# Two pairs of PSUM banks that change places from image to image, and a GpSimd wait on VectorE, in a Winograd convolution block

## What is computed

```python
residual = x
out = conv3x3_decomposed(x, lsq_quantize(w1, alpha1))
out = jax.nn.relu(batchnorm(out, gamma1, beta1))
out = conv3x3_decomposed(out, lsq_quantize(w2, alpha2))
out = batchnorm(out, gamma2, beta2)
out = jax.nn.relu(out + residual)
```

## Time and profile before

| | |
|---|---|
| median of three runs | 1583.57 us (1582.01 to 1583.88) |
| the profiled execution | 1582.83 us, its span 1580.7 us |
| TensorE busy | 1112.5 us, 70% |
| VectorE busy | 1196.5 us, 76% |
| ScalarE busy | 842.3 us, 53% |
| GpSimd busy | 497.5 us, 31% |
| the steps | from 37.5 us to about 1265 us |
| the last stage | about 1265 us to the end |

### The profile page before, as it was taken

One profiled execution on the slowest core, in us unless ns is written; L12 is line 12 of the kernel. 1 busy time (PEld: TensorE's weight loads), 2 busy tenths in 40 slices (PEclk: granted clock), 3 DMA queues, 4 the chain that ended last, 5 costly groups with the idle time before them and its releaser, 6 DMA issues.

```text
span 1580.7 us, 22063 instructions
## 1 busy us (share of the span) xinstructions
PE 1112.5 (70%) x6954; PEld 1058.9 (67%) x6954; DVE 1196.5 (76%) x2074; ACT 842.3 (53%) x1135; POOL 497.5 (31%) x219
## 2 busy tenths in 40 slices
PE   5788998999999999579889999999989900000000
PEld 5787888888888888578888888888888900000000
DVE  7898998888888887688888888888888662323234
ACT  3454555555555555466766777776676552222224
POOL 2343334444433334133344444333344300000000
PEclk9998999999999999799999999999999955555555
DMA  4244444444442220001134444444222199999999
GB/s 191 84 164 161 164 163 163 163 163 180 181 182 107 81 81 1 1 41 82 81 122 163 163 183 180 177 184 189 103 81 81 51 419 430 429 430 430 430 430 407
DMA packets 28103, 296.89 MB, mean 188 GB/s; under 512 B 3888, under 2 KB 3888, under 8 KB 4784
## 3 DMA queue, kind: packets, MB, share of 16 engines
q1 hardware_dynamic: 22608, 245.25, 39.3%
q10 hardware_dynamic: 5472, 51.38, 7.6%
HBM read 174.59 MB, written 122.03 MB: 188 GB/s over the span
## 4 chain that ended last, share of the span: by engine, by line
DVE 42%; DMA 16%; PE 14%; issue 10%; DVEq 3%; ACT 2%; POOL 0%; POOLq 0%; ACTq 0%
PE conv_psum L942 13%; DMA slots<-conv_spill 10%; DVE slots L764 10%; DVE q_rows L696 8%; DVE v_rows L733 4%; DVE p_rows L721 4%; DVE d_lo L737 3%; DMA out<-slots 3%; DMA xbuf<-in_x 3%; DVE conv_psum L756 3%; DVE d L696 2%; DVE v_rows L696 2%; DVE slots L923 1%; DVE v_rows L717 1%; DVEq L764 1%
## 5 line engine op out<-in xcount | busy, mean ns | idle before, releaser
L454 POOL TENSOR_TENSOR v_lo<-v_rows,v_hi 128x1120 fp32r<-128x1120 f32 x192 | 494.9, 2592 | 751.8 <-ACT v_hi L513 751.8
L942 PE MATMUL conv_psum<-v_hi,w1T 128*128 128x284 f32 x1152 | 314.4, 301 | 69.2 <-DVE slots L764 62.5
L942 PE MATMUL conv_psum<-v_hi,w2T 128*128 128x284 f32 x1152 | 312.2, 299 | 66.5 <-DVE slots L764 58.9
L942 PE MATMUL conv_psum<-v_lo,w1T 128*128 128x284 f32 x1152 | 311.7, 299 | 0.0
L942 PE MATMUL conv_psum<-v_lo,w2T 128*128 128x284 f32 x1152 | 309.5, 297 | 0.0
L942 PEld LDWEIGHTS conv_psum<-v_hi,w1T 128*128 128x128 f32 x1152 | 222.0, 193 | 76.4 <-issue 70.5
L942 PEld LDWEIGHTS conv_psum<-v_hi,w2T 128*128 128x128 f32 x1152 | 220.7, 192 | 73.4 <-issue 63.2
L526 ACT COPY m<-conv_psum 128x568 f32<-128x568 f32 x128 | 81.3, 635 | 297.6 <-PE conv_psum L942 297.6
L556 ACT ACTIVATE squares<-slots,minus_shift 128x1120 bf16 (+3 forms) x192 | 223.5, 1164 | 28.8 <-DVE slots L764 15.1
L942 PEld LDWEIGHTS conv_psum<-v_lo,w1T 128*128 128x128 f32 x1152 | 222.6, 193 | 0.0
L942 PEld LDWEIGHTS conv_psum<-v_lo,w2T 128*128 128x128 f32 x1152 | 221.1, 192 | 0.0
(11 more groups left out here) (78 smaller groups left out, 1567.4 us busy)
## 6 DMA issues: line engine op xcount, KB each, us to landing
conv_spill<-slots SPq DMA_DIRECT2D x44, 1568.0 KB, 6.1
slots<-conv_spill SPq DMA_DIRECT2D x44, 1568.0 KB, 10.7
slots<-in_x SPq DMA_DIRECT2D x31, 1568.0 KB, 8.9
out<-slots ACTq DMA_DIRECT2D x30, 1568.0 KB, 11.6
xbuf<-in_x SPq DMA_DIRECT2D x28, 1568.0 KB, 52.8
xbuf_w<-in_x SPq DMA_DIRECT2D x4, 1568.0 KB, 51.9
out<-slots ACTq DMA_DIRECT2D x4, 784.0 KB, 10.3
slots<-in_L_conv_w SPq DMA_DIRECT2D x2, 576.0 KB, 9.7
```

The source lines that it names most:

```text
L454: nc.gpsimd.tensor_tensor(pair_window(1, k), pair_rows(k), pair_window(0, k).bitcast(F32), ALU.subtract).then_inc(lo_ready[k], 1)
L942: last = nc.tensor.matmul(bank_run(M_BANK[k] + grp, G_TILES), w[:, M_WEIGHT[k] + kw, :], run(v_plane[half][k // 2], r0, r0 + G_TILES, kw - 1),
```

## The change

`M_BANK` becomes a list for even images (b = 0) and one for odd ones (b = 1), and the chunks have no banks of their own list any more:

| banks (first of two) | k=0 | k=1 | k=2 | k=3 | k=4 | k=5 | chunks of the next image |
|---|---|---|---|---|---|---|---|
| before, every image | 2 | 4 | 6 | 0 | 4 | 6 | 2, 3 |
| after, even image | 2 | 4 | 0 | 6 | 4 | 2 | 2, 3 |
| after, odd image | 6 | 4 | 0 | 2 | 4 | 6 | 6, 7 |

So product 5 of image g and product 3 of image g + 1 now share banks, where product 5 shared them with product 2 before; and the chunks and product 5 of one step share banks. TensorE's waits follow: product 0 waits for the last sum of the image before, product 2 for nothing in PSUM, product 3 for outer row 1 of the image before and for the evacuation of its chunks; product 5 waits for the evacuation of the chunks just computed instead of for the last sum of its own image (in the last step of a convolution, for the copy of product 0). The transposes of the second weights all wait for the last sum of step 31. And in its loop GpSimd waits, before the low part of pair 2 of image g, until VectorE has made the low part of the direct rows of image g + 1.

```diff
-    M_BANK = [2, 4, 6, 0, 4, 6]
-    CHUNK_BANK = [2, 3]
+    M_BANK = [[2, 4, 0, 6, 4, 2], [6, 4, 0, 2, 4, 6]]
...
+        def chunk_bank(b, j):
+            return M_BANK[1 - b][0] + j
...
                 with pool.Fori(k * IMAGES, (k + 1) * IMAGES - 1) as g:
+
+                    pool.wait_ge(direct_lo_ready, g + 2)
                     lo_of_pair(g, 2)
                     lo_of_pair(g + 1, 0)
                     lo_of_pair(g + 1, 1)
...
                     if k == 0:
                         pe.wait_ge(lo_ready[0], g + 1)
-
-                        pe.wait_ge(evac_done, g * NC + NC)
                     if k == 2:
                         pe.wait_ge(lo_ready[1], g + 1)
+                    if k == 3:
+
+                        pe.wait_ge(evac_done, g * NC + NC)
                     if not first_step:
 
+                        if k == 0:
+                            pe.wait_ge(sums_ready, g * SR)
                         if k == 1:
                             pe.wait_ge(outer_rows_ready, g * OR - 2)
-                        if k == 2:
+                        if k == 3:
                             pe.wait_ge(outer_rows_ready, g * OR)
-                        if k == 3:
-                            pe.wait_ge(sums_ready, g * SR)
-                    product(g, w, k).then_inc(m_done, 1)
-
-            def outer_products(g, w):
+                    product(g, b, w, k).then_inc(m_done, 1)
+
+            def outer_products(g, b, w, last=False):
                 pe.wait_ge(lo_ready[2], g + 1)
-                for j in range(2):
-
-                    pe.wait_ge(sums_ready, g * SR + (2, SR)[j])
-                    product(g, w, QUAD + j).then_inc(outer_done, 1)
+
+                pe.wait_ge(sums_ready, g * SR + 2)
+                product(g, b, w, QUAD).then_inc(outer_done, 1)
+
+                if last:
+                    pe.wait_ge(m_copied, g * 2 + 1)
+                else:
+                    pe.wait_ge(evac_done, g * NC + 2 * NC)
+                product(g, b, w, QUAD + 1).then_inc(outer_done, 1)
...
-            pe.wait_ge(m_copied, IMAGES * 2 - 1)
-            transpose_lot(1, 0)
-            transpose_lot(1, 1)
             pe.wait_ge(sums_ready, IMAGES * SR)
-            transpose_lot(1, 2)
+            for h in range(3):
+                transpose_lot(1, h)
```

More of the change, by code:

```diff
@@ L525, in take_m @@
                 act.wait_ge(m_done, g * QUAD + (2 * j + 1))
-                nc.scalar.copy(grouped((m1, m3)[j][:, :]), group_runs(M_BANK[2 * j])).then_inc(m_copied, 1)
+                nc.scalar.copy(grouped((m1, m3)[j][:, :]), group_runs(M_BANK[b][2 * j])).then_inc(m_copied, 1)
             def take_chunk(g, p, b, j):
@@ L739, in lo_direct, with first_difference @@
                                         ALU.subtract).then_inc(direct_lo_ready, 1)
-            m2, m3_banks, m4 = (group_runs(M_BANK[k]) for k in (1, 2, 3))
+            m2, m3_banks, m4 = ([group_runs(M_BANK[b][k]) for b in range(2)] for k in (1, 2, 3))
             d, s = grouped(d1[:, :]), grouped(s1[:, :])
-            def first_difference(g):
+            def first_difference(g, b):
                 at_least(outer_rows_ready, g * OR)
@@ L779, in outer_row @@
                 dve.wait_ge(sums_ready, g * SR + (SR - 1 + j))
-                row(g, p, b, (0, 3)[j], M_BANK[QUAD + j], 1.0, (s1, d1)[j], outer_rows_ready)
+                row(g, p, b, (0, 3)[j], M_BANK[b][QUAD + j], 1.0, (s1, d1)[j], outer_rows_ready)
             def add_totals(g, b, phase, last=False):
@@ L935, in transpose_lot, with product @@
                 last.then_inc(transposed, 1)
-            def product(g, w, k):
+            def product(g, b, w, k):
                 for grp in range(GROUPS):
@@ L941, in product @@
                             r0 = (k % 2) * TILES + grp * G_TILES
-                            last = nc.tensor.matmul(bank_run(M_BANK[k] + grp, G_TILES),
+                            last = nc.tensor.matmul(bank_run(M_BANK[b][k] + grp, G_TILES),
                                                     w[:, M_WEIGHT[k] + kw, :],
@@ L986, in chunk @@
                     for half in range(2):
-                        last = nc.tensor.matmul(bank_run(CHUNK_BANK[j], r1 - r0),
+                        last = nc.tensor.matmul(bank_run(chunk_bank(b, j), r1 - r0),
                                                 w[:, kh * 3 + kw, :],
@@ L991, in chunk, with chunks, convolve @@
                 last.then_inc(chunk_done, 1)
-            def chunks(g, w):
+            def chunks(g, b, w):
                 for j in range(NC):
[L995 to L1001, removed]
+                    chunk(g, b, j, w)
+            def convolve(g, b, w):
+                inner_products(g, b, w)
+                chunks(g + 1, 1 - b, w)
+                outer_products(g, b, w)
             pe.wait_ge(ident_ready, 1)
@@ L1008, in _ @@
             pe.wait_ge(pads_ready, PADS)
-            chunk(0, 0, wT[0])
+            chunk(0, 0, 0, wT[0])
             pe.wait_ge(w_int_ready[0], 2)
@@ L1012, in _ @@
             transpose_lot(0, 3)
-            chunk(0, 1, wT[0])
+            chunk(0, 0, 1, wT[0])
             pe.wait_ge(wT_ready, TAKES)
-            convolve(0, wT[0])
-            convolve(1, wT[0])
+            convolve(0, 0, wT[0])
+            convolve(1, 1, wT[0])
             with pe.Fori(1, IMAGES // 2 - 1) as i:
                 for b in range(2):
[L1019 to L1022, removed]
+                    convolve(i * 2 + b, b, wT[0])
+            convolve(IMAGES - 2, 0, wT[0])
+            inner_products(IMAGES - 1, 1, wT[0])
+            outer_products(IMAGES - 1, 1, wT[0], last=True)
             pe.wait_ge(w_int_ready[1], 2)
-            pe.wait_ge(m_copied, IMAGES * 2 - 1)
-            transpose_lot(1, 0)
-            transpose_lot(1, 1)
             pe.wait_ge(sums_ready, IMAGES * SR)
-            transpose_lot(1, 2)
+            for h in range(3):
+                transpose_lot(1, h)
             pe.wait_ge(wT_ready, 2 * TAKES)
-            chunks(IMAGES, wT[1])
+            chunks(IMAGES, 0, wT[1])
             with pe.Fori(IMAGES // 2, IMAGES - 1) as i:
                 for b in range(2):
[L1035 to L1038, removed]
+                    convolve(i * 2 + b, b, wT[1])
+            convolve(STEPS - 2, 0, wT[1])
+            inner_products(STEPS - 1, 1, wT[1])
+            outer_products(STEPS - 1, 1, wT[1], last=True)
 _INS = ["x", "L0_conv_w1", "L0_conv_alpha1", "L0_conv_gamma1", "L0_conv_beta1",
```

34 lines of the change are left out of this document (17 added, 17 removed).

## The result

The changed kernel takes **1482.89 us** in the median of four runs (1482.71 to 1483.09), the kernel before 1583.11 us beside it (four runs): a ratio of 0.9367 [0.9351, 0.9384], 100.2 us less. The forecast was 1484. Its profiled execution has a span of 1480.8 us, against 1580.7.

A forecast was written before the change was run, and what follows sets the result against it. Steady steps were taken as bound by a ring of waits between TensorE and VectorE, the last stage by transfers. Savings of 68.2, 12.8, 7.6, 6.3 and 5.0, in all 99.9 us, gave 1482.9, plus 0.7 for the median: 1484 us, range 1470 to 1505.

The forecast's parts named there:

- What would show it: The prediction's list of signs in the trace after the change that would show it right or wrong.
- the first rival: Steady steps: the second ring doesn't bind; step 17.20 us, 7 us more saved, 1477 us; chance 0.22.
- stretched v_rows pair: Two VectorE v_rows operations, 1.40 us together in a steady step, took 5.61 in step 0; predicted to go.
- half clock: TensorE's products 2 and 3 after a stand: 5.53 us instead of 3.24; 2.3 us, twice, in steps 0 to 9.
- items 1, 4 and 5: Savings: 48 steady steps 68.2 us; last two steps of each convolution 6.3; product 5 of steps 31 and 63, 5.0.
- item 2: Steps 0 to 9: 12.8 us saved together, 2.5 of it from the bank change.
- second ring: Steady step: VectorE's L737 1.15, GpSimd's low parts 7.13, VectorE's L785 to L737 8.93, handovers 0.09 and 0.05; 17.35 us, binds.
- from L785 to L737: VectorE's part of the steady step with both inputs in SBUF, taken to exclude GpSimd's operations: 8.93 us.
- first ring: Steady step, VectorE and TensorE through outer row 1: one product (1.57 us) less, from 18.77 to 17.20 us.
- extra operations: Small additional VectorE operations in steps 0 to 9; those of steps 0 and 3 would now meet GpSimd, costing 1.4 us each.
- 8.5 + 4.6 - 2.8: Steps 0 to 9, us: GpSimd no longer among v_rows 8.5, half clock avoided 4.6, extra operations meeting GpSimd -2.8.
- It only starts earlier, so what the steps save is saved whole: Last stage, 315 us, bound by transfers: same bytes after the change, so all savings in the steps reach the end.

The follow-up runs named there:

- the banks alone: The changed kernel without GpSimd's new wait: 1499.64 us, ratio 0.9484.
- GpSimd later: The changed kernel with GpSimd waiting for outer row 1 in all steps but the first of each convolution: 1512.97 us, ratio 0.9558.
- the wait alone: The kernel before, old banks kept, with GpSimd's new wait added: 1567.7 us, ratio 0.9901.

## Why the prediction was right

The direction and the mechanism were right: with its wait back at product 2 the kernel loses 82.7 us again. Of the signs in "What would show it" those in words are in the trace, but the numbers are not: the steady steps are 17.22 and 17.25, below the 17.3 to 17.4 named and nearer to the 17.2 that stood for the first rival, and the two waits are smaller (0.34 to 0.38 for VectorE, 0.16 to 0.24 for TensorE, where 0.4 or 0.5 stood). The stretched v_rows pair named for step 33 belongs to step 32; step 33 had the half clock behind it. The time is within 1.1 us, but this is in part luck: three terms were mis-sized (items 1, 4 and 5) and cancel, and in item 2 the wrong ones cancel within.

1. **Steady steps, 68.2: measured 73.5.** The step is 17.24, not 17.35. All terms of the second ring but one held: from L742's end to GpSimd's start 0.15 (0.09 + 0.05 were taken), three low parts 7.11 (7.13). The one that failed is VectorE's part, 8.93 "from L785 to L737" behind GpSimd's end. L790 starts at 318.34, 0.17 ahead of the end at 318.51, and L738 at 318.46, 0.05 ahead of it; from there to the next L742 it is 8.86. 1.30 + 7.11 - 0.05 + 8.86 = 17.22. L790, held inside GpSimd's run, doesn't take its 0.07 (from its start to the next one's) behind it, and L738 starts 0.05 ahead of the end: 0.12 less together. The rule of the Trainium skill ("SBUF — State Buffer", section "Who interferes with whom") was thus right: the runs agree that whole operations exclude each other, in the 3.33 us of `d_lo` (the banks alone) and in the 0.96 us of a 13-element sum (GpSimd later). The forecast's way of putting it, that the step is then the ring of whole records, was a tenth too much. The step lies nearer to the first rival's 17.20, and a part of that rival's reason holds (VectorE goes on 0.05 before GpSimd's row ends). But its conclusion doesn't: the second ring still binds. The runs with an earlier and a later GpSimd show 17.18 for the first ring and 0.06 on top from the second.
2. **Steps 0 to 9, 12.8: measured 12.7, with errors in it that cancel.** The extra operations met GpSimd in all nine steps, not only in 0 and 3: L279 went from 0.81 to 2.51 and the one of step 3 from 0.55 to 2.31, and the seven others, which had met it before too, gained 0.3 each: 5.6 us, not 2.8. The prediction's terms for the wait sum to 10.3 (8.5 + 4.6 - 2.8), and the run with the wait alone has 9.4; the banks, by which alone that kernel differs from the changed one, give 3.4 more instead of 2.5. Of these, 2.9 lie in steps 1 and 4, where TensorE with the wait alone still stood for 2.72 us and still fell to the half clock behind it (granted clock 0.66 from 57 to 62 us), and VectorE waited for it:

```profile
60.96 0.76 DVE L757 TENSOR_TENSOR conv_psum<-m,conv_psum 128x568 f32<-128x568 f32 x1 [1.28 <-PE conv_psum L943]
...
120.59 0.75 DVE L757 TENSOR_TENSOR conv_psum<-m,conv_psum 128x568 f32<-128x568 f32 x1 [1.42 <-PE conv_psum L943]
```

   In the changed kernel there is no such wait in these steps. So 2.9 of the 4.6 us that the prediction put down to the half clock came only with the banks. Without the wait the banks gave nothing here, since the collisions came back with them.
3. **Steps 32 and 33, 7.6: measured 7.6.** The run with the wait alone has 4.4 of it, and the banks alone 4.6; the two overlap by 1.4.
4. **The last two steps of each convolution, 4 x 1.57 = 6.3: measured 3.2.** The gain came only in steps 30 and 62, where TensorE waits for outer row 1 of the step before (1.69 and 1.74 before the change, 0.18 and 0.24 after it). In steps 31 and 63 no such wait shows in either trace: the ring isn't closed there. Timeline of VectorE in step 31 of after:

```profile
586.19 0.75 DVE L754 TENSOR_TENSOR d<-m,conv_psum 128x568 f32<-128x568 f32 x1 [2.45 <-PE conv_psum L947]
...
589.30 0.75 DVE L761 TENSOR_TENSOR conv_psum<-m,conv_psum 128x568 f32<-128x568 f32 x1 [1.71 <-PE conv_psum L947]
```

   VectorE has little to do there and waits for TensorE already at the first difference; the second comes 3.11 later, two products, as it did before (631.13 to 634.24). The prediction counted four gains and there are two.

5. **Product 5 of steps 31 and 63, 2 x 2.5 = 5.0: measured 3.0.** Step 31 gave 2.6. Step 63's operations behind it also came 2.6 sooner (from its first difference to the affine of the last stage 13.79 us instead of 16.44), but from there to the end it is 307.1 us instead of 304.9: the last stage waits for its transfers. VectorE's wait there, before and after:

```profile
DVE slots L923 <- DMA slots<-conv_spill: 176.8, 22, 11.5
```

```profile
DVE slots L928 <- DMA slots<-conv_spill: 179.6, 22, 11.5
```

   "It only starts earlier, so what the steps save is saved whole" thus holds for what is saved up to step 62, when the transfers are themselves sooner; it failed for what is saved between the last product and the first affine. That the reloads had been issued before and set the end of the stage is argued from these waits, and borne out by the run in which step 63's wait came back and two thirds of it or more didn't reach the end. The 0.4 us of the table are no more than two executions of one kernel differ there.

6. **Transposes and loads, 0.** The steady DMA share is 0.39 as forecast, and no wait on a load shows in steady steps.

The sum is 12.7 + 73.5 + 4.2 + 7.6 + 1.6 + 0.4 = 100.0: +5.3 in item 1 against -3.1 in item 4 and -2.0 in item 5.

## What to carry to other kernels

When no engine is full, follow the ring of waits and count the work that stands in it between the release and the wait. A product takes 1.57 us. Moving a wait behind one took 1.53 off each steady step here, and 1.58 once GpSimd's ring was out of the way; splitting the wait by bank brought the step down to the next ring, 0.24 lower. For two engines that exclude each other, place the start of the second just behind, or just inside, the last operation that it may not meet: 0.7 us later cost 0.73 in each step, one operation earlier gained 0.06 (here, where GpSimd's data comes only while `d_lo` already runs), and no fixed place at all cost 16.7 us in total. Just ahead of a stage that is bound by transfers, a gain on the engines hardly reaches the end.

## What was not expected of the hardware

**The clock fell after a stand that had cost nothing in other steps.** In the run with the wait alone, TensorE stood 1.74 us in step 36, restarted at 738.54, and from 740.07 on its matmuls began 0.236 us apart instead of 0.131, 1.2 instead of 2.4 GHz. The steps around it in the second convolution have the same stand, 1.73 to 1.75, in this kernel and in the kernel before, and kept the whole clock. Windows of that kernel, the granted clock ahead of the DMA share:

```profile
720.00:738.00 18.00, 16.79 (x108) 15.98 (x107) 15.60 (x30) 13.15 (x18) 6.37 (x4) 1.00 0.22 90
738.00:757.00 19.00, 18.46 (x108) 17.75 (x108) 14.98 (x31) 12.00 (x17) 6.96 (x3) 0.91 0.20 85
```

```profile
740.07 0.42 PE L943 MATMUL conv_psum<-v_lo,w2T 128*128 128x284 f32 x1
740.29 0.44 PE L943 MATMUL conv_psum<-v_hi,w2T 128*128 128x284 f32 x1
```

The step took 20.17 us instead of 18.79. Why in this step and not in its neighbours stays open. In step 31 a stand of 3.03 us likewise had three outcomes: all matmuls of product 5 slow before the change, the last few with product 5's wait put back, none with the wait alone. The changed kernel, whose stands are 0.2 us, showed no fall in its steady steps.

**A very small operation on two SBUF inputs pays like a large one:** 13 elements, 0.17 us by themselves, took 0.96 beside GpSimd. In the changed kernel and in "GpSimd later" the held operation ends 0.03 us after GpSimd's run, and VectorE's next one is recorded as starting 0.05 us before its end; in rings a tenth of a microsecond apart this decides which binds.

**Two SBUF inputs are not needed for it.** The prediction counted only operations with both inputs in SBUF. The extra operation of step 1 (L282 before, L285 in the next rows) reads one, and takes 0.76 us where GpSimd starts behind it (GpSimd later), but 2.50 in the changed kernel:

```profile
73.95 0.76 DVE L285 TENSOR_SCALAR slots<-slots 128x1152 f32<-128x1152 f32 x1
```

```profile
74.86 2.50 DVE L285 TENSOR_SCALAR slots<-slots 128x1152 f32<-128x1152 f32 x1
```
